# A decoder layer on one core: maxima of the second attention as stack rows, sums of the first attention turned in SBUF

## What is computed

```python
x = _layernorm(x + _L0_attn_ref(x, ...))             # self-attention, 16 heads of 8 features
x = _layernorm(x + _L0_xattn_ref(x, ctx, ctx, ...))  # attention to the context, 16 heads
x = _layernorm(x + _L0_ffn_ref(x, ...))              # 16 experts, the 4 best weighted
```

```python
scores = jnp.einsum('bhqd,bhkd->bhqk', q, k) * SCALE
esc = jnp.einsum('bhqd,bhkd->bhqk', eq, ek) * (1.0 / math.sqrt(HD)) * decay
attn = jax.nn.softmax(scores + ENT * esc, axis=-1)
ctx = jnp.einsum('bhqk,bhkd->bhqd', attn, mixed)
```

## Time and profile before

| | |
|---|---|
| median of 3 runs | 363.0 us (362.45 to 364.02) |
| profiled execution | 365.59 us |
| its span, first to last instruction | 363.8 us |
| TensorE / VectorE / ScalarE / GpSimd busy | 91% / 71% / 60% / 59% |
| mean granted clock of TensorE | 0.978 |
| DMA queue of SP: packets, MB | 67328, 52.43 |

### The profile page before, as it was taken

One profiled execution on the slowest core, in us unless ns is written; L12 is line 12 of the kernel. 1 busy time (PEld: TensorE's weight loads), 2 busy tenths in 40 slices (PEclk: granted clock), 3 DMA queues, 4 the chain that ended last, 5 costly groups with the idle time before them and its releaser, 6 DMA issues.

```text
span 363.8 us, 11400 instructions
## 1 busy us (share of the span) xinstructions
PE 332.0 (91%) x3536; PEld 256.6 (71%) x3536; DVE 257.2 (71%) x1220; ACT 218.7 (60%) x522; POOL 215.0 (59%) x401
## 2 busy tenths in 40 slices
PE   8987989999999979896799999999799999999993
PEld 5766777877787758775678788888556765666662
DVE  1686888999999988875457776769945269345454
ACT  3785778999998866684586766756453252212120
POOL 8475789998888874876753334321125355464552
PEclk9998999999999998998899999999999999999998
DMA  7799899798998895947355757561046220444310
GB/s 232 174 304 239 220 235 238 177 208 200 196 208 186 208 204 107 255 95 150 76 126 106 156 127 140 126 138 46 2 136 202 77 60 0 142 128 131 128 32 29
DMA packets 67807, 54.06 MB, mean 149 GB/s; under 512 B 29616, under 2 KB 57648, under 8 KB 67632
## 3 DMA queue, kind: packets, MB, share of 16 engines
q1 hardware_dynamic: 67328, 52.43, 60.4%
q10 hardware_dynamic: 432, 1.05, 0.9%
HBM read 33.40 MB, written 20.05 MB: 147 GB/s over the span
## 4 chain that ended last, share of the span: by engine, by line
PE 51%; issue 13%; DVE 11%; ACT 9%; POOL 6%; DMA 5%; SPq 3%; ACTq 0%; POOLq 0%; DVEq 0%
PE bank L838 7%; PE bank L1106 5%; PE bank L1110 4%; PE bank L1119 4%; DMA parts_dram<-parts 3%; PE bank L792 3%; PE bank L821 3%; PE bank L814 3%; PE bank L731 3%; PE bank L781 3%; PE bank L763 2%; PE bank L771 2%; PE bank L851 2%; DMA stk<-parts_dram 2%; ACT parts L1217 2%
## 5 line engine op out<-in xcount | busy, mean ns | idle before, releaser
L1526 DVE CUSTOM_DVE_ANT_0 bank<-bank,decayed_e 128x128 f32<-128x128 f32 x256 | 67.2, 325 | 0.5
L697 POOL TENSOR_TENSOR stk<-stk 128x512 f32<-128x512 f32 x32 | 40.7, 1271 | 38.5 <-ACT stk L1442 35.8
L1537 DVE TENSOR_REDUCE top<-bank 128x4 bf16<-128x512 f32 x64 | 43.9, 687 | 19.5 <-PE bank L792 19.3
L1234 ACT ACTIVATE prob_t<-bank 128x512 f32<-128x512 f32 x64 | 38.8, 606 | 27.9 <-PE bank L821 27.6
L1442 ACT ACTIVATE stk<-bank 128x512 f32<-128x512 f32 x32 | 19.1, 597 | 53.6 <-PE bank L1106 53.6
L1781 DVE TENSOR_TENSOR stk<-bank,stk 128x512 f32<-128x512 f32 x32 | 22.0, 691 | 39.1 <-POOL stk L697 38.0
L1224 ACT ACTIVATE prob<-bank 128x512 f32<-128x512 f32 x64 | 39.2, 613 | 16.3 <-PE bank L771 16.0
L838 PE MATMUL bank<-prob_t,vmix 128*32 128x128 f32 x1024 | 43.6, 283 | 5.5 <-ACT pvs L1258 5.5
L1514 DVE TENSOR_TENSOR decayed_e<-bank,decay 128x512 f32<-128x512 f32 x64 | 44.0, 688 | 4.4 <-issue 4.3
L499 POOL TENSOR_TENSOR rest<-pf,parts 128x256 f32<-128x256 f32 (+1 forms) x31 | 28.1, 906 | 27.7 <-ACT parts L1213 27.7
L505 POOL TENSOR_TENSOR parts<-rest,parts 128x256 bf16<-128x256 f32 (+1 forms) x31 | 28.1, 906 | 25.9 <-ACT parts L1217 25.9
(11 more groups left out here) (172 smaller groups left out, 781.1 us busy)
## 6 DMA issues: line engine op xcount, KB each, us to landing
stk<-parts_dram SPq DMA_DIRECT2D x32, 384.0 KB, 5.4
stk<-shares_dram SPq DMA_DIRECT2D x64, 128.0 KB, 3.0
parts_dram<-parts SPq DMA_DIRECT2D x32, 192.0 KB, 3.1
parts_dram<-parts SPq DMA_DIRECT2D x48, 128.0 KB, 2.8
stk<-parts_dram SPq DMA_DIRECT2D x32, 192.0 KB, 3.5
parts_dram<-parts SPq DMA_DIRECT2D x32, 96.0 KB, 2.9
parts_dram<-parts SPq DMA_DIRECT2D x48, 64.0 KB, 2.1
w<-in_w_dram SPq DMA_DIRECT2D x3, 512.0 KB, 5.5
```

The lines of the kernel that those rows point to most:

```text
L697: pool.tensor_tensor(h1[kk % 2], sg[kk % 2], share[kk], ALU.mult).then_inc(weighted, 1)
L1234: act.activation(prob_t[g][:].rearrange("p h t -> p (h t)"), bank[2 + g % 2][:], ACT.Exp).then_inc(L2.exped, 1)
L1526: m = dve.tensor_tensor_reduce(out=bank[g % 2][:, 128 * j:128 * j + 128], in0=bank[g % 2][:, 128 * j:128 * j + 128], in1=decayed_e[:, g % ...
L1537: dve.tensor_reduce(top[:, b.par, GH * g:GH * g + GH], bank[S2_BANK[g % 2]][:].rearrange("p (h t) -> p h t", h=GH), AX.X, ALU.max).then_in ...
```

## The change

Three parts.

1. **First attention.** L1526 writes its sums to a new SBUF tile (sums) instead of back to PSUM. turn is now one step: four transposes of sums into bank 3, then four products of 128 columns that subtract the maxima there. exponent reads bank 3 and writes prob_t; the copy take_turned, the tile prob and one pipeline step are gone.
2. **Second attention.** The second product of score_t is gone. Instead the stack has 16 more rows, partitions 96 to 111. On the key side they hold, for the whole run, minus a constant near 1 where the row is the head's own and zero elsewhere (pick_rows, two loads at the start). On the query side top_row, one more transfer of SP per batch, writes top_t into them, each row repeated for all heads; clear_row on GpSimd sets them to zero again before the buffer's next score2. The 48 other rows now lie on every second partition, 0 to 94. score2, VectorE's maximum2 and turn_top come earlier (score2 by three units), turn_top uses bank 4, and SP's order is new and written out for all batches: spill runs three batches ahead.
3. **Waits and order.** ScalarE's wait at (14, 0) for both spill buffers becomes one wait for each of two batches, one unit later. x_tok is loaded later, and GpSimd's base and residual_bias pieces are spread over more slots.

```diff
-        prob = [sb(f"prob{p}", [128, GH, S]) for p in range(2)]
+        sums = [sb(f"sums{p}", [128, GH, S]) for p in range(2)]
...
+            def pick_rows(p):
+
+                sp.wait_ge(zeroed[p], 1)
+                keys = stk[p][:].rearrange("p a h u t -> p (a h u t)").bitcast(F32)[TOP_ROW:TOP_ROW + H, H * S:2 * H * S]
+                sp.dma_start(keys.rearrange("p (k n) -> p k n", k=2),
+                             k["pick_rows"].unsqueeze(1).broadcast_to([H, 2, H * S // 2])).then_inc(in_rows_k, 16)
...
-                sp.dma_start(dst[0:R, :, at:at + H // 2], src[:, :, at:at + H // 2]
+                sp.dma_start(dst[0:2 * R:2, :, at:at + H // 2], src[:, :, at:at + H // 2]
...
-                    sp.dma_start(stk2[b.buf][0:R, side], src[side]).then_inc(L2.stacked[b.buf], 16)
+                    sp.dma_start(stk2[b.buf][0:2 * R:2, side], src[side]).then_inc(L2.stacked[b.buf], 16)
+
+            def top_row(b):
+
+                sp.wait_ge(L2.top_t_ev, b.n + 1)
+                sp.dma_start(stk2[b.buf][TOP_ROW:TOP_ROW + H, 0],
+                             top_t[0:H, b.par, :].unsqueeze(1).broadcast_to([H, H, S])).then_inc(L2.topped[b.buf], 16)
...
-            spill(L2, Batch2(0, 0))
+            spill(L2, slot_batch(0))
             load_ffn()
-            quad2(0)
-            with sp.Fori(1, 3) as q:
-                quad2(q)
-            quad2(3)
+            spill(L2, slot_batch(1))
+            stack2(slot_batch(0))
+            spill(L2, slot_batch(2))
+            for s in range(NB + 1):
+                if s + 1 < NB:
+                    stack2(slot_batch(s + 1))
+                if s >= 1:
+                    top_row(slot_batch(s - 1))
+                if s + 3 < NB:
+                    spill(L2, slot_batch(s + 3))
...
+            def clear_row(b):
...
+                pool.wait_ge(L2.shifted, NG * b.n + NG)
+                pool.memset(stk2[b.buf][TOP_ROW:TOP_ROW + H, 0].rearrange("p h t -> p (h t)").bitcast(F32), 0.0
+                            ).then_inc(L2.row_zero, 1)
...
             def slot2(b):
+                c = b.back(3)
+                if c.live and c.n < NB - 4:
+                    clear_row(c)
+                    pool.wait_ge(L2.row_zero, c.n + 1)
...
-            def subtract_max(b, g):
+            def turn(b, g):
                 u = b.n * NG + g
                 pe.wait_ge(L1.maxed, u + 1)
...
                 if not isinstance(u, int) or u >= 1:
-                    pe.wait_ge(L1.turned_ev, u)
+                    pe.wait_ge(L1.exped, u)
                 for j in range(GH):
-                    t = pe.transpose(bank[3][:, 128 * j:128 * j + 128], prob[g % 2][:, j, :], ident[:])
-                t.then_inc(L1.turned, 1)
+                    pe.matmul(bank[3][:, 128 * j:128 * j + 128], sums[g % 2][:, j, :], ident[:], start=(j == 0), stop=True,
+                              is_transpose=True, skip_group_check=True)
+                for j in range(GH):
+                    m = pe.matmul(bank[3][:, 128 * j:128 * j + 128], shift[:, g % 2, j:j + 1].broadcast_to([128, 128]),
+                                  neg_ident[:], start=False, stop=True, skip_group_check=True)
+                m.then_inc(L1.turned, 1)
...
                 if g == 0:
                     pe.wait_ge(L2.stacked[b.buf], b.quad * L2.stack_step + L2.stack_step)
+                    if not isinstance(b.n, int) or b.n >= 4:
+                        pe.wait_ge(L2.row_zero, b.n - 3)
...
+                if g == 0:
+                    pe.wait_ge(L2.topped[b.buf], b.quad * 16 + 16)
                 for j in range(GH):
...
-                for j in range(GH):
-                    h = GH * g + j
-                    m = pe.matmul(bank[2 + g % 2][:, 128 * j:128 * j + 128],
-                                  neg_ident[:, h:h + 1].broadcast_to([128, 128]), top_t[:, b.par, :],
-                                  start=False, stop=True, skip_group_check=True)
+                    m = pe.matmul(bank[2 + g % 2][:, 128 * j:128 * j + 128], stk2[b.buf][:, 1, head(g, j), :],
+                                  stk2[b.buf][:, 0, head(g, j), :], start=True, stop=True)
...
-                sb_, sg_ = unit_back(bb.back(1), g, -2)
+                sb_, sg_ = unit_back(bb.back(1), g, -5)
...
+                act.wait_ge(L1.turned, u + 1)
...
+                act.activation(prob_t[g][:].rearrange("p h t -> p (h t)"), bank[3][:], ACT.Exp).then_inc(L1.exped, 1)
...
-                    for p in range(2):
-                        act.wait_ge(L1.spilled[p], NB // 2 * L1.spill_step)
...
                     if g == 1:
+                        if b.n < 2:
+                            act.wait_ge(L1.spilled[b.par], NB // 2 * L1.spill_step)
                         high(L2, b, False)
...
-                            out=bank[g % 2][:, 128 * j:128 * j + 128], in0=bank[g % 2][:, 128 * j:128 * j + 128],
+                            out=sums[g % 2][:, j, :], in0=bank[g % 2][:, 128 * j:128 * j + 128],
...
+        "pick_rows": _np.repeat(-1.0058441162109375 * _np.eye(H), S // 2, 1),
```

More of the change, by code:

```diff
@@ L324, in build @@
         RT_STEPS = 22
+        TOP_ROW = 96
         WARM = 10
@@ L407, in _ @@
             spill(L1, Batch(0, 0))
-            sp.wait_ge(zeroed[0], 1)
+            pick_rows(0)
             stack1(Batch(0, 0), 0)
@@ L411, in _ @@
             spill(L1, Batch(0, 1))
-            sp.dma_start(x_tok[:].rearrange("p b n -> p (b n)"), k["x_tok"]).then_inc(in_xt, 16)
-            sp.wait_ge(zeroed[1], 1)
+            pick_rows(1)
             stack1(Batch(0, 1), 0)
@@ L660, in slot2, with last_slot1 @@
                     lowest(L2, b.back(-3))
-            def first_parts2(k):
-                remainder(L2, Batch2(0, k))
-                lowest(L2, Batch2(0, k))
-            slot1(7, 0)
-            pool.wait_ge(L1.low, NB)
-            first_parts2(0)
-            slot1(7, 1)
-            residual_bias(0, 8)
-            first_parts2(1)
-            slot1(8, 0)
-            first_parts2(2)
-            slot1(8, 1)
-            slot2(slot_batch(0))
-            slot1(9, 0)
+            def last_slot1(n, parts):
+                b = Batch(n // 2, n % 2)
+                if b.back(5).live:
+                    gain_and_sum(b.back(5))
+                if b.back(4).live:
+                    inverse_root(b.back(4), 0)
+                if parts is not None:
+                    remainder(L2, parts)
+                if b.back(1).live:
+                    mix_values(b.back(1))
+                if b.back(5).live:
+                    inverse_root(b.back(5), 1)
+                if parts is not None:
+                    lowest(L2, parts)
+            pool.wait_ge(L1.low, NB)
+            for n in range(14, 17):
+                last_slot1(n, Batch2(0, n - 14))
+            last_slot1(17, Batch2(0, 3))
+            residual_bias(0, 4)
+            last_slot1(18, None)
             slot2(slot_batch(1))
+            residual_bias(4, 8)
+            last_slot1(19, None)
+            slot2(slot_batch(2))
             residual_bias(8, 12)
-            slot1(9, 1)
-            slot2(slot_batch(2))
-            slot1(10, 0)
+            last_slot1(20, None)
             slot2(slot_batch(3))
@@ L684, in _ @@
             slot2(slot_batch(4))
-            with pool.Fori(1, 3) as q:
-                for i4 in range(1, 5):
-                    slot2(Batch2(q, 0).back(-i4))
-            for n in range(13, NB + 4):
+            for n in range(5, NB + 4):
                 slot2(slot_batch(n))
@@ L883, in unit1 @@
                     turn_out(L1, b3, TAIL1)
-                for lag, stage in ((1, subtract_max), (2, turn)):
-                    ub, ug = unit_back(b, g, lag)
-                    if ub.live:
-                        stage(ub, ug)
+                ub, ug = unit_back(b, g, 1)
+                if ub.live:
+                    turn(ub, ug)
                 if g == 1 and b3.live:
@@ L901, in unit2 @@
                     project2(bb.back(-3))
-                sb_, sg_ = unit_back(bb.back(1), g, -2)
+                if g == 0 and isinstance(bb.n, int) and bb.n == 0:
+                    score2(bb, 0)
+                sb_, sg_ = unit_back(bb.back(1), g, -5)
                 if sb_.live:
                     score2(sb_, sg_)
+                if g == 0 and isinstance(bb.n, int) and bb.n == 1:
+                    turn_top(bb.back(1))
                 tb = bb.back(2)
@@ L914, in unit2 @@
                     out_product(L2, bb.back(4), xw_t[:, 3, :])
-                if g == 2 and bb.back(1).live:
-                    turn_top(bb.back(1))
+                if g == 3 and bb.live and (not isinstance(bb.n, int) or bb.n >= 1):
+                    turn_top(bb)
                 if g == 3 and bb.back(3).live:
@@ L1309, in unit2 @@
             def unit2(bb, g):
-                if g == 3 and bb.back(1).live:
+                if g == 0 and bb.back(1).live:
                     take_top(bb.back(1))
@@ L1655, in unit2 @@
                     residual(L2, bb.back(4), TAIL2)
```

(4 more changed lines are left out.)

143 lines of the change are left out of this document (64 added, 79 removed).

## The result

| | before | with the change |
|---|---|---|
| median | 362.9 us (4 runs) | 377.6 us (4 runs, 377.38 to 377.73) |
| ratio, 95% interval | 1 | 1.040 (1.0375 to 1.0424) |
| span of the profiled execution | 363.8 | 375.9 |

The change makes the kernel 4.0% slower, 14.7 us. The forecast was 355.0, its range 348 to 367.

The account below looks back on a forecast made before the run. It took the first attention as full on all engines, VectorE nearest its end, the second as TensorE's until SP's loop stood next. Terms -3.0 - 2.0 - 4.4 + 1.0 + 2.4 - 2.0 = -8.0 took the median 363.0 to 355.0 us, range 348 to 367.

Parts of the forecast that it names:

- the loop through SP: Second attention: exponential, middle part, lowest part, spill, stack loads, score2 in a round; 6.0 us, bounds 5.6 and 7.0.
- Nine slots at 6.0: Second attention: nine batch places at 6.0 us each against 5.73 before, +2.4 us (-1.2 to +11.4).
- Slow clock: Second attention: TensorE idling 2.2 us a slot drops its clock to 0.50 and lengthens the loop's pieces, +1.0 us.
- rival 1: Second attention: stack loads land no sooner, loop 7.0 us, clock falls; 366.5 us, slower; chance 0.19.
- Slots 0 to 4: Second attention's first five slots: GpSimd finishes both layers' work plus clear_row's memset, some showing, +1.0 us (0 to +3).
- Last four slots: End of second attention: no spill left, 0.88 us less each, part kept by VectorE's routing; -2.0 us (0 to -3.5).
- Start: Kernel start: x_tok behind batch 1's stack loads gives back a TensorE wait and slow clock, -3.0 us (0 to -4.5).
- First attention: First attention: ScalarE loses a copy, VectorE stands next, its idle 0.29 us a batch gained over seven batches, -2.0 us.
- Hand-over: Between the attentions: ScalarE's spill wait later and halved, GpSimd's addition cut into later halves; -4.4 us (-2 to -5.5).
- Rival 3: Second attention: the loop closes early, TensorE bounds slots at 4.85 us; 344.7 us; chance 0.08.
- Rival 2: First attention stays, GpSimd bounding it; start and hand-over give 3 of 9.4; 361.4 us; chance 0.15.
- rival 4: Second attention: maxima come too late, SP waiting for a spill ahead of them; +10, 365 us; chance 0.06.

Follow-up runs that it names:

- e2: The change with the 48 stack rows of both attentions back on adjacent partitions 0 to 47: 388.8 us, 1.070 of the kernel before.
- e1: The change with each batch's stack loads issued by SP before the middle and lowest parts of the next batch's spill: 356.8 us, 0.982 of the kernel before.
- e3: The change with clear_row's memset cut from 1024 to 16 numbers per partition: 377.8 us, 1.043 of the kernel before.
- e11: e1 with GpSimd's eight additions as 3, 3, 2 in three places and the top rows' load issued by ScalarE: 354.15 us, 0.973 of the kernel before.
- e12: e11 with the first clear_row earlier in GpSimd's list, ahead of an addition and the first attention's last steps: 354.2 us, 0.971 of the kernel before.
- e5: The kernel before with only x_tok loaded later and GpSimd's additions spread: 366.4 us, 1.007 of the kernel before.
- b2: The kernel before, unchanged, executed a second time under the profiler: 361.8 us, span 360.0.
- e6: The kernel before with only the first attention's part (sums in SBUF, no copy take_turned): 361.7 us, 0.996 of the kernel before.
- e4: The kernel before with only ScalarE's wait for both spill buffers made one wait per batch, a unit later: 359.8 us, 0.992 of the kernel before.
- e13: e12 with x_tok's load and GpSimd's eight additions where the kernel before has them: 354.9 us, 0.975 of the kernel before.
- e8: e1 with the 48 stack rows back on partitions 0 to 47: 359.7 us, 0.993 of the kernel before.

## Why the prediction was wrong

The forecast's mechanism was right: it named the loop through SP link by link, as the thing that would stand next. Its size and reach were not, and one more term had the wrong sign. The result lies 22.7 us above the forecast: in the traces 10.1 of them are the loop's eight slots, 6.0 the last four, 2.5 slots 0 to 4 and 2.0 the first attention, less 0.5 at the start, and 2.6 are the profiled execution's distance from the median.

- **Nine slots at 6.0: +2.4.** This is the step that failed. The slots took 7.29 in the mean, above even its upper bound of 7.0. Of the loop's links, the landing was put at 2.45 and measured at 3.27. It came from 384 KB divided by rates of the earlier trace rows, as if these bytes moved alone and at the weight loads' rate; the spread does shorten it, by 0.5 to 0.7 us (e2). The start of that subtraction was off too: without the spread the second load of a pair lands after 4.02 us in this loop (e2), where the sum had 3.5. The bound left out that an issue of SP can itself be long: in the round shown above the landing (+0.82) and GpSimd's start to L382 (+0.59) make up the whole 1.4 us above 6.0. On the row at 211.13 the issue is 0.93 where 0.47 is usual, and it goes to 1.7:

```profile
247.60 1.71 SPq L379 DMA_DIRECT2D parts_dram<-parts  x1
...
DMA packets 13, 0.02 MB, mean 32 GB/s; under 512 B 12, under 2 KB 12, under 8 KB 12
## 3 DMA queue, kind: packets, MB, share of 16 engines
q8 instruction: 1, 0.02, 14.0%
```

  (SP's row, and the DMA of 247.5 to 248.1, with one packet of instructions.) Four of the eight slots have such an issue inside the loop (of 0.93 to 1.95 us).
- **Slow clock.** Taken only in rival 1. Seven stretches at 0.50, of 3.4 or 6.8 us, lie between 162 and 262 us, each in or just behind a gap of TensorE of 1.4 us or more; four of them lie in the eight slots. They lengthen what TensorE does in the loop. What this adds to it no run tells apart.
- **Slots 0 to 4: +1.0**, measured +3.5. The loop already turned there, which the sum didn't count: with it cut, e1 takes 27.7 us for 29.2. The memset's length, which was what I priced, is 0.6 us in e3's trace and nothing in its median. The cause of the other 2.0 us stays open: in the change the longest wait, 4.30 us up to 178.43, is ended by a stack load behind a spill's issue of 1.86 us, 0.4 us after clear_row's end; in e11 the wait there is ended by clear_row, and with clear_row earlier (e12) the slots still take 27.2.
- **Last four slots: -2.0**, measured +4.0. "No spill is left" is not so at their start: batch 15's middle part goes out at 247.19, and loads follow it. The loop still made the slots that start at 240.16 and 247.06, the second 8.4 us long, and the slower clock behind a wait of 3.53 us then met the router's 16 products (L1075, 3.43 us; 1.86 before). With the loop cut (e1) this piece is 35.5 us for 40.0, still only 0.4 below the 35.9 of before.
- **Start: -3.0.** -3.5 between the two traces, but +2.5 by e5's ratio. The step took the stall of one execution for a property of the kernel, though that execution stood 2.6 us above the median, as I had written; 2.1 us of it were gone in b2, and e5 waits 1.93 us for the next load instead. And "their sum is the same: 0" was wrong for the moved additions: one a slot, 1.27 us on a GpSimd with less than 1 us to spare, builds up until VectorE waits:

```profile
81.78 0.29 DVE L1630 BATCH_NORM_STATS2 stats<-res 128x6 f32<-128x128 f32 x1 [1.52 <-POOL res L587]
...
83.96 0.33 PE L896 MATMUL bank<-ident,attn_o 128*128 128x128 f32 x1 [0.87 <-DVE attn_o L1642]
```

- **First attention: -2.0**, measured -1.3 alone (e6) and 0.0 within the change, which loses its gain in the slot of 9.1 us. The reason given was wrong: VectorE did get cheaper, and TensorE took its place. The comparison of two rows of 290 ns took the first of four; the mean was 325 and fell to 287.
- **Hand-over: -4.4**, -4.4 in the traces and -3.0 in the medians (e4, ScalarE's wait alone). Right; but 1.5 us was again the clock of that execution (b2), so that the size came out is in part luck.
- **Rivals.** The first (loop 7.0, slow clock, slower) is nearest to what happened, with too small a price: 366.5 for 377.6. Its premise, that the loads land no sooner, was false (e2); the loop was long all the same. It multiplied nine slots where TensorE waited for a stack load in 13, and kept most of the other gains. Rival 3's premise, an early close, was false in the change, and is what e1 builds. Rival 2 is nearer than the forecast for the start and the first attention in the medians (+2.5 and -1.3 where -5.0 was forecast), but TensorE and not GpSimd became the fullest engine there. Of rival 4 nothing shows: the waits name no load of the top rows. The prediction's chance of 0.19 for slower is too low by its own terms: rivals 1 and 4, less their tenth, add up to 0.22.

## What to carry to other kernels

When a transfer's consumer is moved earlier, follow the queue order from the consumer back: here a load whose data had been ready for a slot stood behind the wait of another batch's spill, and turning two entries of the list was worth 21 us. A load of 384 KB that lands after 3 us is not priced by its bytes over a rate read elsewhere: take the landing of its like, beside the same transfers. A stall in one profiled execution that stands above the median is not money in hand: take a second execution, or discount it, before a change is credited with it.

The best version found keeps the change's idea: stack loads ahead of the spill, top rows on ScalarE's queue (e11, 0.973, with e12 and e13 not to be told from it).

## What the runs showed that I had not expected

- All six issues of SP above 0.9 us between 187 and 256 us have one 16 KB packet of the instruction queue near them, from 0.1 us behind to 0.7 us ahead of their start, and there are no other such packets in that stretch. Whether that is the cause was not tried; in the kernel before, six of the nine such packets of the same stretch have no long issue beside them.
- Issuing a load to every second partition takes SP 0.52 and 0.59 us, to adjacent ones 0.41 and 0.42 (e2) or 0.32 and 0.42 (e8); it matters once SP is full.
- An instruction of VectorE that reads PSUM and writes SBUF was 38 ns shorter in the mean than the one that writes PSUM, and its accumulator's read 58 ns (e6).
- The same kernel's two profiled executions differed by 3.8 us: 2.0 by batch 0 and 1.6 more by slot 0, both where the first had a clock of 0.50 for 3.4 us behind a gap (of 1.85 and of 2.23 us) and the second, behind gaps of 1.30 and 2.17, kept 1.00. The length of the gap alone didn't decide it.
